# GpSimd waits for each group of eight gathers before it issues the next, in two of four edge stages

## What is computed

```
L0: score = exp(leaky(s_src[src] + s_dst[dst]) - max), per head (4)
    out   = segment_sum(proj[src] * score / segment_sum(score))
L1: out   = layernorm(relu(x W_self + b + segment_mean(x[src] W_msg)))
L2: alpha = softmax over the edges of one source of leaky(ei[dst] + ej[src])
    out   = relu(segment_sum(alpha * x[src], dst))
L3: out   = x W + b + segment_max(x[src] W[edge type] + b[edge type], dst)
```

## Time and profile before

| | |
|---|---|
| median of three runs, no profile | 4590.77 us |
| span of the profiled execution | 5974.2 us |
| GpSimd busy in it | 3220.8 us (54%), 3391 instructions |
| TensorE busy | 2467.8 us (41%) |
| VectorE busy | 2086.7 us (35%) |
| ScalarE busy | 830.0 us (14%) |

### The profile page before, as it was taken

One profiled execution on the slowest core, in us unless ns is written; L12 is line 12 of the kernel. 1 busy time (PEld: TensorE's weight loads), 2 busy tenths in 40 slices (PEclk: granted clock), 3 DMA queues, 4 the chain that ended last, 5 costly groups with the idle time before them and its releaser, 6 DMA issues. The chain is left out here.

```text
span 5974.2 us, 63099 instructions
## 1 busy us (share of the span) xinstructions
PE 2467.8 (41%) x16441; PEld 2221.3 (37%) x16441; DVE 2086.7 (35%) x5443; ACT 830.0 (14%) x2496; POOL 3220.8 (54%) x3391
## 2 busy tenths in 40 slices
PE   2344444444333333332766666454566222222221
PEld 1333333333233333331666666344455222222220
DVE  4344434444122222222444344355544122222223
ACT  0111212122000000000322222000001011001112
POOL 3555555554566666664344444545443666666664
PEclk7555555555555555555555555566666556555555
DMA  4222222222122222223333333455555344434443
GB/s 102 57 60 60 61 58 60 59 61 57 41 47 47 47 49 47 48 47 63 115 110 108 107 108 115 130 162 162 162 164 160 93 117 116 108 108 112 112 116 82
DMA packets 427122, 543.15 MB, mean 91 GB/s; under 512 B 116266, under 2 KB 291966, under 8 KB 426862
## 3 DMA queue, kind: packets, MB, share of 16 engines
q1 hardware_dynamic: 311618, 311.80, 17.7%
q0 software_dynamic: 108064, 223.63, 16.6%
q10 hardware_dynamic: 7344, 6.61, 0.4%
HBM read 403.82 MB, written 142.41 MB: 91 GB/s over the span
## 5 line engine op out<-in xcount | busy, mean ns | idle before, releaser
L523 POOL DMA_INDIRECT G<-table,IC x2496 | 2362.6, 947 | 1571.7 <-issue 832.5
L2412 POOL DMA_INDIRECT G<-table,IC x448 | 433.1, 967 | 580.9 <-ACT IC L2271 425.1
L2818 DVE TENSOR_TENSOR_SCAN GW<-BIG,GW,PS 128x512 f32<-128x512 bf16 x208 | 266.2, 1280 | 962.9 <-DMA BIG<-run_mask 620.8
L2412 POOL DMA_INDIRECT G<-table2c,IC x384 | 367.3, 956 | 407.0 <-DMA rows_ahead<-G 148.8
L2780 PE MATMUL PS<-IDENT,GW 128*128 128x128 f32 x840 | 192.5, 405 | 862.3 <-issue 481.4
L1360 PE MATMUL PS<-SEL,G 128*128 128x96 f32 x1664 | 372.1, 417 | 358.1 <-DVE SEL L556 217.1
L1032 PE MATMUL PS<-SEL,GW 128*128 128x96 f32 x1664 | 382.4, 419 | 291.6 <-DVEq L1095 158.9
L1360 PEld LDWEIGHTS PS<-SEL,G 128*128 128x128 f32 x1664 | 359.7, 327 | 365.5 <-DVE SEL L556 220.1
L2780 PEld LDWEIGHTS PS<-IDENT,GW 128*128 128x128 f32 x840 | 158.9, 215 | 887.3 <-issue 495.6
L1032 PEld LDWEIGHTS PS<-SEL,GW 128*128 128x128 f32 x1664 | 356.4, 322 | 304.3 <-DVEq L1095 165.3
L2426 PE MATMUL PS<-BIG 128*128 128x49 f32 x1680 | 387.4, 408 | 60.7 <-issue 31.8
(11 more groups left out here) (314 smaller groups left out, 3749.1 us busy)
## 6 DMA issues: line engine op xcount, KB each, us to landing
rows_ahead<-G SPq DMA_DIRECT2D x104, 520.0 KB
running_max<-BIG SPq DMA_DIRECT2D x105, 512.0 KB
G<-table,IC POOLq DMA_INDIRECT x2944
GW<-source_in_block SPq DMA_DIRECT2D x160, 256.0 KB
ROWSF<-edge_places SPq DMA_DIRECT2D x209, 192.0 KB
BIG<-run_mask SPq DMA_DIRECT2D x104, 256.0 KB
ROWSF<-rows_ahead SPq DMA_DIRECT2D x26, 520.0 KB
SELTF<-rows_ahead SPq DMA_DIRECT2D x26, 520.0 KB
```

The costliest lines, as they stand in the source:

```text
L523: pool.indirect_dma_start(out=G[:, b, u, 0:width], out_offset=None, in_=table, in_offset=bass.IndirectOffsetOnAxis(ap=IC[:, b * U + u:b * ...
L2412: pool.indirect_dma_start(out=GS[:, b, u, 0:width], out_offset=None, in_=table, in_offset=bass.IndirectOffsetOnAxis(ap=IC[:, b * U + u:b * ...
L2818: v.tensor_tensor_scan(RM[:, q, h * 512:(h + 1) * 512], MB[:, q, h * 512:(h + 1) * 512], PS[2 * q + h][:], before, ALU.min, ALU.max).then_ ...
```

## The change

`gather_rows` gets a parameter `settle`, which `edges0` alone sets (`edges1` and two other stages that call it don't). With it, and always in `gather_turns` of `layer2`, GpSimd waits after the eight gathers of a group until `gathered[b]` has counted all of them.

```
-        def gather_rows(pool, table, width, indices_ready, opened, gathered, used, ahead):
+        def gather_rows(pool, table, width, indices_ready, opened, gathered, used, ahead, settle=False):
             with pool.Fori(0, passes(pool)) as pss:
...
                         pool.wait_ge(indices_ready, number(pss, turn, b) + 1)
                         pass_wait(pool)
                         gather_group(pool, table, width, b, gathered)
+                        if settle:
+                            pool.wait_ge(gathered[b], turn * (16 * U) + 16 * U)
+                            pass_wait(pool)
...
-                    gather_rows(pool, T0, D + H, ic_ready, opened, gathered, rows_used, 0)
+                    gather_rows(pool, T0, D + H, ic_ready, opened, gathered, rows_used, 0, settle=True)
...
                             for u in range(U):
                                 pool.indirect_dma_start(
                                     out=GS[:, b, u, 0:width], out_offset=None, in_=table,
                                     in_offset=bass.IndirectOffsetOnAxis(
                                         ap=IC[:, b * U + u:b * U + u + 1], axis=0)).then_inc(gathered[b], 16)
+                            pool.wait_ge(gathered[b], turn * (16 * U) + 16 * U)
+                            pass_wait(pool)
```

## The result

The changed kernel takes 5154.78 us (median of 3 runs, 5151.72 to 5158.76), the kernel before 4590.77 us (4589.56 to 4595.85) on the same chip: a ratio of 1.120, with a 95% interval of 1.113 to 1.127. The change costs 564 us where 369 were forecast. The direction was forecast rightly, the time lies above the range of 4780 to 5060 us. The step that failed is the price of one wait: 2.1 us, at most 2.4, were put on record, and it came out at 2.7 us in `edges0` and at 2.4 and 3.4 us in the two gather loops of `layer2`.

What follows compares the result with a forecast made beforehand. It took GpSimd's gather issue to bound the runs in nearly every edge stage. 208 waits at 2.1 us are 437 us, less 50 slack, less 15 at `layer2`'s end: 372 on 4591, said as 4960 us, range 4780 to 5060.

Steps and rivals of the forecast that it cites:

- price of one wait: At each group end of `edges0` and `layer2`: 2.1 us more until the next gather, bounds 1.4 and 2.4 us.
- floor of 4160 us: GpSimd's least time to issue all 416 gather groups of the four edge stages, at 10.0 us a group.
- (a): At a group's end, the last gather's start to its landing, read from a waiting reader's start: 2.63 to 2.90 us.
- (b): After a wait, the time until released GpSimd starts its next gather: 0.79 us, read behind an index copy.
- The slack: GpSimd's pauses that absorb waits: 34 to 111 us in all four stages, 50 us of it given to the changed two.
- The end of `layer2`: Work trailing the last gather of `layer2` has caught up when GpSimd is later, giving back 15 us.
- its plan slips: Sign of error in `layer2`: SyncE, held in `spill`, loads rows late, TensorE stands, costing more than its share of 208 us.
- full price and more: Rival: late landings in `layer2`, 3.2 us a group there, and no slack: 551 us more, 5140 us; chance 0.07.
- Hidden: Rival: runs have the trace's pauses in proportion and the waits fall into them: 4591 us; chance 0.05.
- partly hidden: Rival: waits in the changed stages partly fall into pauses, or `edges0` alone pays: 4820 or 4810 us; chance 0.18.
- Faster: Rival: SyncE's small loads in `edges0` land sooner during the pauses, 1 us won a group: 4487 us; chance 0.02.
- the profiled span should hardly grow: Sign: the profiled span grows much less than the runs; `edges0`'s group period there, 13.4 us, exceeds GpSimd's 10.0 + 2.1.

Runs made afterwards that it cites:

- x12: The kernel before, unchanged, profiled on a chip of the first kind: 4578.97 us.
- x1: The kernel before, unchanged, profiled again on a chip of the second kind: 6051.75 us.
- x11: The changed kernel with the wait added to `edges1` and `edges3` too, first kind of chip: 5691.17 us, 1.241 of the kernel before.
- x9: The changed kernel with the wait behind every second group only, first kind of chip: 4845.38 us, 1.056 of the kernel before.
- x10: The changed kernel with a queue drain and twenty semaphore raises instead of each landing wait, first kind of chip: 5449.28 us, 1.188 of the kernel before.
- x15: The kernel before with half a row per gather in `edges0`, `edges1` and `edges3`, and a clearing of G, second kind of chip: 6032.53 us, 0.999.
- x14: The changed kernel with a drain and twenty semaphore raises instead of each landing wait, second kind of chip: 5890.02 us, 0.975 of the kernel before.
- x5: The changed kernel itself, run again on a chip of the second kind: 5588.5 us, 0.934 of the kernel before.

## Why the prediction was right, and where it was wrong

**What bounds the kernel: right for the runs, with a wrong reason for the profile.** The prediction held the floor of 4160 us against the median and concluded that the runs are bound by the issue. The windows of `x12` show it: 1055 to 1059 us in three stages of 1040 us of issue, 1163 in the third. The assumption that a gather costs 1.25 us in a run too holds to the digit. But the profile read did not differ from the runs because it was a profile; it came from a chip on which this kernel takes 6000 us in any run (`x1`). The rule "the change costs what it costs the issue" was true for the one kind of chip and would have been false for the other, where the sign is the opposite. That the result was measured on the first kind is luck as far as the direction goes: the prediction had no case for two kinds of chip.

**The price of a wait: the step that failed.** It was put at 2.63 to 2.90 us for (a) and 0.79 for (b), less one reader's start counted twice, less 1.25: 2.1 us, at most 2.4. By the profile's pages above, busy and idle time of the gathers grew by 279 us for the 104 groups of `edges0`, by 137 us for the 56 groups of `layer2`'s first loop (448 gathers) and by 164 us for the 48 of its second: 2.7, 2.4 and 3.4 us a wait, 580 us in all. In `edges0` the mean from the last gather of a group to the next gather is 3.84 us where 3.35 were forecast; the rest of the 2.7 is in the spacings within groups.

`x11` shows the two parts apart, because its trace has the landings of some groups. GpSimd starts its next gather 0.93 to 0.97 us after the landing of the last one, in `edges0` and in `edges1` alike. The last gather of a group lands 2.46 us after its start in `edges1`, in the mean of the slot b = 0, and 3.44 us after it in the one slot of `edges0` that is known, b = 1 (single ones 2.5 to 3.9). This is the view of all known landings in `edges0`, most of them of earlier gathers of a group:

```profile
DMA to landing us min/median/max: 2.4/2.5/3.9
```

So an undisturbed group end takes 2.46 + 0.94 = 3.40 us, and the forecast of 3.35 was right for it. It is about what the changed kernel's groups b = 0 and 2 of `edges0` take (medians 3.53 and 3.47 us), while b = 1 and 3 take 4.42 and 3.95, and the two gather loops of `layer2` 4.50 and 4.68 in the mean. The error was to take two group ends of unchanged stages as the mean of the changed ones, with a late landing in `layer2` seen and left out of the mean. Why the last gather of those groups lands about 1 us later isn't shown.

The Trainium skill's sum on "DMA: Bandwidth & Descriptors", section "Anatomy of one DMA — SWDGE (gpsimd) path", gave an estimate of 2.16 us to the landing. The trace of `x11` has a median of 2.5 us and no landing under 2.4, and the price of 1.7 us that followed from the estimate is further off than the rows' 2.1.

**The slack: about as forecast.** 50 us were given to the changed stages, of 34 to 111 us in all four. In `x12` the four stretches from first to last gather are 4253 us in all, 93 more than 4160, and 87 of them are in `layer2`; `edges0` has none. In `layer2` the gathers have 310.5 us of idle time before them; 832 times 0.30 are 250, the first indices took 20.7, and 40 are left, 31.1 of them in one wait. Most of the rest of the 87 is slower issue (1043 ns mean in the first loop against 948 on line 523), which no wait can fall into. `x9` gives an estimate of 42 us from the other side. The 580 us above are what is left after this slack; before it they would be some 622, 3.0 us a wait (an estimate from the two).

**The end of `layer2`** was to give back 15 us. The pauses add 301 us there and the stage is 292 us longer, so it gave back 9. The 292 us are more than the forecast had for this stage, which the prediction named as a sign that its plan slips; but GpSimd's own gaps account for all of it, so it isn't one here.

**The sum.** Forecast 437 less 50 less 15 = 372. The terms as measured are 580, with the slack in it already, less 9: 571 us, against 564 between the medians and 579.7 between the two spans. The rival "full price and more" (5140 us, 3.2 us a group in `layer2`, no slack) comes nearest, at a chance of 0.07, but by luck: its 2.1 us in `edges0` is too low, its 3.2 in `layer2` is above the 2.9 that the 104 waits cost there net, and the slack that it denies is there in `layer2`.

**The other rivals.** Hidden and partly hidden are excluded on this kind of chip by `x9`, `x10` and `x11`: the pauses cost their length in each stage, but for some 40 us in `layer2`. Faster is not: it is the result on the second kind. The mechanism that was named for it, small loads that land sooner, is not shown. `x15`, with half the bytes, changed nothing, and `x14`, which waits for no landing, gained, so the gain hangs on GpSimd's pause, and outside `layer2` not on the gathers' bytes. Whether loads stand behind the gathers' many small transfers, whose number `x15` keeps, wasn't tested.

**What the profile was to show.** 3.35 us from the last gather to the next in both stages: 3.52 and 4.33 in the rows, 3.84 in the mean of `edges0` and 4.57 in that of `layer2`, against 1.25 in the unchanged ones. GpSimd's idle time ends on its own gathers' landing at 78 of the 103 group ends of `edges0`, after, first kind (us, times, longest):

```profile
POOL G L523 <- issue: 310.3, 753, 3.5
POOL G L523 <- DMA G<-table,IC: 222.5, 78, 3.8
```

The other 25 stand under "issue", whose longest is 3.5 us where it was 0.3: a releaser that the trace didn't tell. The sentence that the profiled span should hardly grow was an argument on the second kind of chip. There it didn't grow but shrank, from 6049.9 to 5583.4 us between `x1` and `x5`, which are of different batches.

**Not settled.** Why two kinds of chips give one kernel 4590 and 6000 us, and what it is in an unbroken run of indirect gathers that holds up the other engines' instructions on the second. The experiments show that a pause in each group of 12 to 14 us shortens the changed stages there and ends TensorE's standing in `edges0`, that a shorter pause gains half and one in 20 us less than a fifth, that a wait for the landing isn't needed, and that outside `layer2` the bytes play no part. In both full pauses, the wait and the drain, every gather has landed before the next is issued, so they don't tell whether it helps that GpSimd issues nothing or that nothing of it is under way. They don't show the place in the chip either.

## What to carry to other kernels

Where an engine issues gathers back to back and the stage's length is their number times their spacing, every wait for a landing costs the whole way from the issue over the landing to the restart, here 3.8 us in `edges0` less the 1.25 of one issue, and it should be read from the mean over many groups of the stage that changes, not from two rows of others. Before a sum is made, hold the profile's span against the runs: where they differ by 30%, as here, the profile may be of other circumstances, and the change has to be thought through in both. Here a wait cost 12% on one chip and was worth 6.5% on another, so the times of such a kernel are to be taken on more than one.

## What the runs showed of the hardware

- The same kernel took 4578.97 to 4595.85 us on some chips and 5960.14 to 6091.8 us on others, at nearly the same busy times (`x12` and `x1`: VectorE 2089.7 and 2085.0 us, GpSimd 3263.1 and 3226.0, TensorE 2398.5 and 2448.7).
- On the second kind, in the kernel whose GpSimd issues gathers without a pause of its own, TensorE's matmuls stood 2.1 us apart in stretches with nothing named that they waited for, 531 us in `edges0`; with a wait of GpSimd in each group of 12.6 us it was 10 us, and the kernel with 208 waits was 6.5% faster than the one without.
- An indirect gather of 128 rows cost GpSimd 1.25 us with whole rows on both kinds of chip, and with half rows on the second (`x15`).
- A gather landed 2.4 us after its start at the least and 2.5 in the median, and the last one of a group in a slot of `edges0` 3.44 in the mean (`x11`). GpSimd, waiting for the landing, started its next gather 0.93 to 0.97 us after it.
- A GpSimd instruction held by a semaphore that the landing raises started 0.83 and 0.92 us behind a VectorE instruction held by the same landing.
